# Slab product waits by node chunk, and convolved slabs stay in a buffer on the chip

## The reference

```
xc = attention over channels(x);  xt = attention over time(xc)
s  = softmax(left @ xt^T / sqrt(dk))             # 512 x 512 per sample
h  = einsum('bnm,bmct->bnct', s * A, xt)         # graph product with adjacency A
y  = relu(conv2d(h @ W_gcn, tcn_w) + conv2d(x, res_w))
z  = (y - mean) / sqrt(var + 1e-5) * ln_g + ln_b # over the 16 output channels
```

## Time and profile before

| | |
|---|---|
| median of three runs | 1605.48 us (1602.06, 1605.48, 1621.79) |
| profiled execution, its own time | 1613.76 us |
| its span, first to last instruction | 1612.0 us |
| PE busy | 1377.9 us (85%) |
| PE weight loads busy | 1145.1 us (71%) |
| DVE busy | 955.3 us (59%) |
| ACT busy | 716.2 us (44%) |
| POOL busy | 591.8 us (37%) |
| mean granted PE clock | 0.895 of 2.4 GHz |
| DMA | 174 MB, mean 108 GB/s |

### The profile page before, as it was taken

How to read it: one execution, slowest core, us unless ns; L and a number is a source line. 1 busy time by engine, 2 the same in 40 slices (tenths; PEclk the granted TensorE clock), 3 DMA queues, 4 the chain that set the end, 5 groups by cost and what they waited for, 6 DMA issues and landing times. The chain is left out here.

```text
span 1612.0 us, 25621 instructions
## 1 busy us (share of the span) xinstructions
PE 1377.9 (85%) x8186; PEld 1145.1 (71%) x8202; DVE 955.3 (59%) x2027; ACT 716.2 (44%) x1227; POOL 591.8 (37%) x904
## 2 busy tenths in 40 slices
PE   5788999999398499999999994677899999936997
PEld 5686888878398488888888783666688788833554
DVE  4403788888444764445544433646278888855985
ACT  5432555555154332333333322522255555524996
POOL 1100365665511246655575432100026556560000
PEclk8798999999656699999999995578799999977999
DMA  7461122212276236554574626874112122212321
GB/s 238 123 194 40 40 69 70 77 59 78 75 237 222 88 111 146 105 116 110 124 148 77 123 26 169 294 254 116 40 33 77 59 78 68 61 57 78 102 76 60
DMA packets 105615, 173.99 MB, mean 108 GB/s; under 512 B 14768, under 2 KB 47168, under 8 KB 105540
## 3 DMA queue, kind: packets, MB, share of 16 engines
q1 hardware_dynamic: 83268, 128.95, 25.7%
q0 software_dynamic: 16384, 31.51, 11.3%
q10 hardware_dynamic: 5888, 12.59, 2.2%
HBM read 106.91 MB, written 66.10 MB: 107 GB/s over the span
## 5 line engine op out<-in xcount | busy, mean ns | idle before, releaser
L929 PE MATMUL g_y<-L_z,L_pt 128*128 128x192 f32 x1024 | 198.4, 338 | 1.5 <-ACT L_pt L1144 0.5
L929 PEld LDWEIGHTS g_y<-L_z,L_pt 128*128 128x128 f32 x1024 | 168.0, 194 | 6.8 <-ACT L_pt L1144 6.8
L1089 POOL TENSOR_TENSOR L_xr<-L_xr,L_lnb 128x192 f32<-128x192 f32 x128 | 105.6, 852 | 171.4 <-DMA L_xr<-x 93.4
L1486 POOL DMA_INDIRECT sums<-x_yo,x_places x64 | 102.9, 1609 | 136.0 <-ACT x_yo L1725 125.9
L1136 ACT ACTIVATE L_e<-g_s,L_nm 128x512 f32<-128x512 f32 x128 | 88.0, 687 | 78.2 <-DVE L_nm L977 77.1
L1096 POOL TENSOR_TENSOR L_t<-L_rstd 128x48 f32<-128x48 f32 x96 | 28.9, 301 | 224.9 <-DVE L_rstd L1031 219.9
L897 PE MATMUL g_z<-L_kw,L_xnT 96*128 96x192 f32 x512 | 91.8, 331 | 20.8 <-DVE L_v L1007 20.5
L897 PEld LDWEIGHTS g_z<-L_kw,L_xnT 96*128 96x128 f32 x512 | 82.3, 189 | 30.0 <-DVE L_v L1007 30.0
L1615 DVE TENSOR_TENSOR x_mid<-ex_g,x_sig 128x480 f32<-128x480 f32 (+1 forms) x48 | 31.4, 654 | 120.2 <-ACT x_sig L1716 120.2
L986 DVE SCALAR_TENSOR_TENSOR L_p<-L_e,L_rl,L_adj 128x512 f32<-128x512 f32 x128 | 99.1, 774 | 4.5
L977 DVE TENSOR_REDUCE L_nm<-g_s 128x1 f32<-128x512 f32 x128 | 87.5, 684 | 22.7 <-PE g_s L906 21.9
(11 more groups left out here) (352 smaller groups left out, 3574.4 us busy)
## 6 DMA issues: line engine op xcount, KB each, us to landing
L_xnT<-xn_rows SPq DMA_DIRECT2D x48, 384.0 KB, 3.4
x<-L_y SPq DMA_DIRECT2D x32, 384.0 KB, 2.9
xn_rows<-L_xnT SPq DMA_DIRECT2D x54, 192.0 KB, 4.1
L_xr<-in_x SPq DMA_DIRECT2D x24, 384.0 KB, 3.5
L_xr<-x SPq DMA_DIRECT2D x24, 384.0 KB, 3.8
L_raw<-xn_rows SPq DMA_DIRECT2D x16, 384.0 KB, 4.9
ff_xa<-x SPq DMA_DIRECT2D x12, 512.0 KB, 4.2
out_x<-ff_yo SPq DMA_DIRECT2D x16, 384.0 KB, 2.6
```

Source lines behind the costliest of these rows:

```text
L929: last = nc.tensor.matmul(out, pt[k % 2][:, P * c:P * c + P], z[q][:, c, :], start=False, stop=(c == NK - 1))
L1089: last = nc.gpsimd.tensor_tensor(v_, v_, gain(s.lnb), ALU.add)
L1486: nc.gpsimd.indirect_dma_start(sums, row(places[e % 2][:, 1, t:t + 1]), yo[t % 4][:, :], None, compute_op=ALU.add).then_inc(sent[t % 4], 16)
```

## The change

- **conv_slab** waits for kw_sb ahead of node chunk 0, and for uv_sb ahead of chunk 2 only.
- **graph_conv** has no output in DRAM. residual writes slab b into s.slabs, a view of s.shared, at columns b x 192 of each node chunk; the address comes from the loop register. The stores, the semaphores sent and the waits for them in residual, relu and at the block's end are gone.
- **normalise** with route on reads the slabs from s.slabs, and has no loads and no waits for them.
- **feed_forward** reads its slabs from s.slabs for the transposes and for its residual. The ring xa, the loads and their waits are gone.
- **build**: x1 and x3 are gone. The shared buffer is made per layer, and in layer 1 outside the convolution's buffers, so that it lives through the feed-forward.

```diff
 # normalise
-        xa = [s.xa0, s.xa1, s.xr0, s.xr1]
+        xa = None if route else [s.xa0, s.xa1, s.xr0, s.xr1]
+        def slab(b, k, h):
+            if route:
+                return s.slabs[:, k, CT * b + HALF * h:CT * b + HALF * h + HALF]
+            return xa[b % 4][:, k, HALF * h:HALF * h + HALF]
...
-                    if b + 4 < B:
+                    if not route and b + 4 < B:
                         load(b + 4)
...
                 def turn_slab(b):
-                    pe.wait_ge(xa_in[b % 4], (b // 4 + 1) * 16)
+                    if not route:
+                        pe.wait_ge(xa_in[b % 4], (b // 4 + 1) * 16)
                     since(pe, xn_done, b - D + 1)
...
-                                                       xa[b % 4][:, k, HALF * h:HALF * h + HALF], s.ident[:, :])
+                                                       slab(b, k, h), s.ident[:, :])
 # graph_conv
                 with sp.Fori(0, B // 2 - 2) as i:
                     for q in range(2):
                         load(i * 2 + q + 3, 1 - q)
-                        store(i * 2 + q, q)
                         load_residual(i * 2 + q + 2, q)
...
-                for q in range(2):
-                    sp.wait_ge(sent[q], dma_ready(B // 2 - 1))
...
                 def conv_slab(b, q):
-                    pe.wait_ge(uv_sb, ready(b))
+                    pe.wait_ge(kw_sb, ready(b))
                     for k in range(NK):
+                        if k == 2:
+                            pe.wait_ge(uv_sb, ready(b))
                         for h in range(2):
...
-                def residual(b, q, i):
+                def residual(b, q):
                     dve.wait_ge(gained, ready(b))
                     dve.wait_ge(base_done, ready(b))
-                    dve.wait_ge(sent[q], dma_free(i))
-                    nc.vector.tensor_tensor(y[q][:, :, :], dv[q][:, :, :], xr[q][:, :, :], ALU.add).then_inc(out_done, 1)
+                    nc.vector.tensor_tensor(s.slabs[:, :, bass.ds(b * CT, CT)], dv[q][:, :, :], xr[q][:, :, :],
+                                            ALU.add).then_inc(out_done, 1)
...
                     act.wait_ge(out_done, free(b, 2))
-                    act.wait_ge(sent[q], dma_free(i))
                     nc.scalar.activation(slab(y[q]), psy[:, :, 0:2 * CT], ACT.Relu).then_inc(relu_done, 1)
 # feed_forward
-        xa = [sb(f"xa{z}", [P, NK, W]) for z in range(RING)]
...
                 def turn_slab(b):
-                    pe.wait_ge(slab_in[b % RING], (b // RING + 1) * 16)
                     since(pe, tn_done, b)
...
-                                                       xa[b % RING][:, k, P * h:P * h + P], s.ident[:, :])
+                                                       s.slabs[:, k, W * b + P * h:W * b + P * h + P], s.ident[:, :])
...
-                            in_time(xa[b % RING][:, :, P * h + at:P * h + at + C * count]), ALU.add)
+                            in_time(s.slabs[:, :, P * n + at:P * n + at + C * count]), ALU.add)
 # build
+    def shared_buffer(ctx, L):
+        s.shared = sb(ctx, f"shared{L}", [P, B * NK * CT])
+        s.slabs = s.shared[:, :].rearrange("p (k x) -> p k x", k=NK)
...
-            graph_conv(nc, s, "g0", rows(xn_rows), by_partition(d["x"]), by_partition(x1))
-            normalise(nc, s, "n1", by_partition(x1), 1e-5, rows(xn_rows), keep=rows(raw_rows))
+            graph_conv(nc, s, "g0", rows(xn_rows), by_partition(d["x"]))
+            normalise(nc, s, "n1", None, 1e-5, rows(xn_rows), keep=rows(raw_rows))
```

More of the change, by code:

```diff
@@ L379, in load @@
                 def load(b):
-                    since(sp, logits_done if route else slab_turned, b - 3)
+                    since(sp, slab_turned, b - 3)
                     sp.dma_start(xa[b % 4][:, :, :], src[b]).then_inc(xa_in[b % 4], 16)
@@ L384, in _ @@
                     consts.first(sp)
-                load(0)
-                load(1)
+                if not route:
+                    load(0)
+                    load(1)
                 if consts:
                     consts.rest(sp)
-                load(2)
-                load(3)
+                if not route:
+                    load(2)
+                    load(3)
                 for b in range(B):
@@ L423, in logits @@
                         for k in range(NK):
-                            last = nc.tensor.matmul(psl[0:HALF, at:at + E], xa[b % 4][:, k, HALF * h:HALF * h + HALF],
+                            last = nc.tensor.matmul(psl[0:HALF, at:at + E], slab(b, k, h),
                                                     s.wr[:, k, :], start=(k == 0), stop=(k == NK - 1))
@@ L781, with graph_conv @@
 CENTRE_STEPS, NORM_STEPS = 3, 6
-def graph_conv(nc, s, tag, xn_rows, x_in, x_out, prefetch=None):
+def graph_conv(nc, s, tag, xn_rows, x_in, prefetch=None):
     with ExitStack() as ctx:
-        (xn_in, xr_in, sent, kron_done, kw_done, kw_sb, uv_done, uv_high, uv_sb, z_done, z_sb,
+        (xn_in, xr_in, kron_done, kw_done, kw_sb, uv_done, uv_high, uv_sb, z_done, z_sb,
          score_done, nmax_done, expd, probs, probs_turned, probs_turned_sb, y_done, relu_done, stats_done,
@@ L795, in graph_conv @@
             tag,
-            "xn_in*2 xr_in*2 sent*2 kron_done kw_done kw_sb uv_done uv_high uv_sb z_done z_sb "
+            "xn_in*2 xr_in*2 kron_done kw_done kw_sb uv_done uv_high uv_sb z_done z_sb "
             "score_done nmax_done expd probs probs_turned probs_turned_sb y_done relu_done stats_done "
@@ L841, in _ @@
                         load(i * 2 + q + 3, 1 - q)
-                        store(i * 2 + q, q)
                         load_residual(i * 2 + q + 2, q)
                 load(B - 1, 1)
[L845 to L848, removed]
-                for q in range(2):
-                    sp.wait_ge(sent[q], dma_ready(B // 2 - 1))
+                for b in range(B - 2, B):
+                    load_residual(b, b % 2)
             def item_turns(eng, turn):
@@ L1059, in turn @@
                     if total:
-                        residual(b - 2, q, i - q)
+                        residual(b - 2, q)
                     if norm:
@@ L1159, in turn @@
                     if norm:
-                        relu(b - 1, r, i)
+                        relu(b - 1, r)
                     if softmax:
@@ L2042, in _ @@
             def _(sp):
[L2043 to L2047, removed]
+                for b in range(B):
                     sp.wait_ge(out_done, last_tile(b) + 1)
                     sp.dma_start(x_out[b], yo[b % SLABS][:, :, :]).then_inc(sent[b % SLABS], 16)
[L2051 to L2054, removed]
-                    while done < B and last_tile(done) <= 2 * c + 1:
-                        store(done)
-                        done += 1
-                    if c + RING < STEPS:
-                        load(c + RING)
                 for z in range(SLABS):
@@ L2469, in build @@
     raw_rows = sums[0:TOKENS, :]
-    x1, x2 = (dram(n, [B, P, NK * CT]) for n in ("x1", "x2"))
-    x3 = dram("x3", [P, NK * TOKENS])
+    x2 = dram("x2", [B, P, NK * CT])
     gate_rows = dram("gate_rows", [3 * TOKENS, 1])
@@ L2532, in build @@
                 small_attention(nc, s, "t1", False)
-                graph_conv(nc, s, "g1", rows(xn_rows), by_partition(x2), x3.rearrange("p (k b x) -> b p k x", k=NK, b=B))
-            feed_forward(nc, s, x3.rearrange("p (k j x) -> j p k x", k=NK, x=2 * P), node_major(out))
+                graph_conv(nc, s, "g1", rows(xn_rows), by_partition(x2))
+            feed_forward(nc, s, node_major(out))
         s.sems.ctx.close()
```

17 lines of the change are left out of this document (7 added, 10 removed).

## The result

The changed kernel took 1554.89 us (median of 4 runs, 1552.27 to 1557.21), the kernel before 1603.77 us beside it (4 runs, 1599.72 to 1621.79): a ratio of 0.967 with a 95% interval of 0.960 to 0.975. The forecast was 1563, the range 1548 to 1586. The profiled execution took 1557.21 us (span 1555.4), 56.6 less than that of before.

| stretch | before, us | after, us | saved | the prediction's term |
|---|---|---|---|---|
| begin of g0 to its last residual | 305.2 | 296.5 | 8.8 | 6.3 |
| last residual of g0 to the begin of n1 | 2.8 | 0.3 | 2.5 | 2.5 |
| n1 to the next block's first issue | 79.7 | 50.9 | 28.7 | 26 |
| n1 to the begin of g1 (unchanged) | 623.2 | 621.4 | 1.8 | 0 |
| begin of g1 to its last residual | 305.0 | 297.0 | 8.0 | 6.3 |

What follows compares the result with a forecast made beforehand. PE was taken as tightest in the turns, and in n1 PE-bound at 1.2 GHz; 12.5 + 2.5 + 26 + 6.9 = 47.9 us off 1613.8 gave 1565.9, less a third of 8.3, 1563 us; range 1548 to 1586.

Steps and rivals of the forecast that it cites:

- The turns: Graph convolution turns, both layers: splitting conv_slab's wait fills PE's gap before the product; 12.5 us saved.
- 12 x 0.42: Steady turns 2 to 13 of a layer: each gains 0.42 us, limited by ACT's copy of probability tile 3.
- Turns 0 and 1: First two turns of each layer's convolution: without residual, each gains the whole 0.61 us.
- the store of 2.5 us: End of layer 0's convolution: without the store's landing the next block begins 0.3 us after the last residual; 2.5 us saved.
- n1, 26 predicted: Row norm without its 16 loads: PE stays at 2.4 GHz, 2.75 us a slab; 26 us saved.
- The granted clock came back some 40 us later: Row norm before the change: after a 3.10 us wait for a load, PE's full clock returned some 40 us later.
- while PE worked through at full pace it kept the clock: Row norm: reason given for PE staying at 2.4 GHz once the waits for loads go.
- cold n1: Rival, row norm: PE stays at 1.2 GHz, 5.2 us a slab, a loss of 5 us; 1594 us, chance 0.06.
- The feed-forward: Its begin: no store to land (3.1 us) and no load before the first transposes (3.8 us); 6.9 us saved.
- The third that I took off: Forecast total: a third of the profiled run's 8.3 us above the median, taking 1565.9 to 1563 us.
- came back at other waits: Rival, turns: PE's 0.68 us return in full at spread(b,3) or projections, the 12.5 us go; 1575 us, chance 0.14.
- Residual by a register's address: Rival, DVE: residual's write in four runs is slow and delays 28 turns; 1619 us at 2.0 more, chance 0.03.

Runs made afterwards that it cites:

- buffer alone: Changed kernel with conv_slab's wait for uv_sb back at its start, so that slabs kept on chip are all that is new: 1570.1 us, ratio 0.978.
- Experiment 1: Kernel before with only conv_slab's wait split: 1587.0 us; changed kernel with the old wait back at conv_slab's start: 1570.1 us.
- experiment 2: Changed kernel with 16 slab loads in n1 that nothing reads: 1565.5 us with PE not waiting, 1584.9 us with PE waiting for each.
- experiment 3: Changed kernel with PE stopped in n1 until an unread 49 KB load lands: once 1568.9 us, three times 1576.8 us.
- experiment 4: Changed kernel without the two products per slab that n1 makes only to keep PE busy: 1571.1 us, ratio 0.977.
- wait alone: Kernel before with one edit, conv_slab waiting for kw_sb at its start and uv_sb ahead of chunk 2: 1587.0 us, ratio 0.987.
- experiment 5: Changed kernel with residual later on DVE 1551.3 us, half of conv_slab earlier on PE 1557.6 us, both 1552.2 us; changed kernel beside the last 1561.0 us.
- bytes alone: Changed kernel with 16 slab loads in n1 that nothing reads and PE does not wait for: 1565.5 us, ratio 0.972.
- one gap: Changed kernel with PE stopped once in n1, behind the logits of slab 4, until an unread 49 KB load lands: 1568.9 us, ratio 0.976.
- loads awaited: Changed kernel with 16 unread slab loads in n1, PE waiting for each before that slab's transposes: 1584.9 us, ratio 0.987.

## Why the prediction was right

**The turns, 12.5 predicted, 16.8 measured: mechanism right, size off in the first turns.** From first to last residual, which the steady turns set, 5.3 and 5.7 us were saved, and the working gives 12 x 0.42 = 5.0 for them. The step that was mis-sized is "Turns 0 and 1 have no residual, so there I take the whole 0.61". In g1, from the product of turn 0 on, two products lay 16.86 us apart before and 15.99 after (1170.00 to 1186.86; 1128.18 to 1144.17): 0.87. PE's idle time of 0.61 leaves out that a product behind a pause takes 2.87 in place of 2.77 us, and that, with no pause, it starts 0.16 us before the modelled end of its predecessor. Turns 0 and 1 so gave 1.8 us a layer and not 1.2. The last 2.3 of the 16.8 us lie ahead of turn 0's split of u, and the change does not explain them: from the begin of the convolution to that split the buffer alone, with the old wait, took 25.1 and 27.9 us in its two layers, the kernel before 27.8 and 27.6, and the changed kernel 26.2 and 27.0. Experiment 1 shows that the wait, and not the store, made the turns' gain. A mean turn of 16.49 us stands against 16.45 predicted. That fit hides a miss: the limit has two parts, spread(b,3), as argued, and row_probs(b,2) behind centre on DVE, which the prediction did not have.

**Residual at 0.95 us, the store of 2.5 us: right** (0.95 and 2.5).

**n1, 26 predicted, 28.7 measured: right, with a slab of 2.70 in place of 2.75 us.** The block took 50.9 us where about 53 was predicted. That the load's wait and not only its bytes made it slow is shown by experiment 2, and that a pause alone ends the 2.4 GHz by experiment 3. Two sentences of the working did not hold. "The granted clock came back some 40 us later" was one execution: other runs had 7 to 44 us. And "while PE worked through at full pace it kept the clock" is true only of the work as it stood. In experiment 4 it fell, without a pause, once transposes and narrow logits were all that PE did, and the whole n1 took 15.9 us more. So the two idle products per slab, which the change left alone, carry about half of what was saved from the last residual of g0 to the end of n1 (15.9 of 31.2 us), and the prediction priced a cold n1 without naming them. The Trainium skill ("TensorE: Matmul & The Clock Gate", "Part 4: PE-mode transpose") says that the full clock does not come on for transposes. Against that page, the clock rose behind the first 24 transposes in the changed kernel and in experiment 4, as in the earlier trace rows; for it speaks the fall in experiment 4, so it bears on this case more than I allowed.

**The feed-forward, 6.9 predicted, 8.1 measured.** The transposes follow the last residual after 0.70 us, where 7.54 passed: 6.8, as worked out. The other 1.3 us lie in the stage itself (158.6 to 157.3 us from the first transposes on) and are no gain of the change: the wait alone, with the old feed-forward, took 157.2 us there.

**The sum.** 1613.8 - 47.9 - 2.8 = 1563; with the terms as measured, 4.3 + 2.7 + 1.2 us less, it is 1554.9, the median. To the tenth that is luck, since the stretches that the change leaves alone moved by 1.3 and 1.8 us. The third that I took off for the profiled execution's excess over the median fits what experiment 1 showed, an n1 that in one execution took 10 us less than in another; that this is the whole of the excess is not shown.

**The rivals.** Of the 0.87 us that a pause cost, only 0.4 came back at other waits in a steady turn. The cold n1 did not come, but experiment 4 shows that it was two products per slab away (67.2 us in place of 51.3). Residual by a register's address cost nothing.

## What to carry to other kernels

A wait that holds a whole group of products back for an operand of half of them can be split, here at no cost that a run shows, but look at what the next engine allows: here a steady turn kept 0.47 of the 0.87 us, and two moves together (experiment 5) freed only 0.2 more. A transfer that PE waits for can cost far more than its length, since the pause can take the clock with it; count the work at 1.2 GHz behind it, from several executions. And before idle products on PE are cut, take the clock's rows with and without them.

## What was unexpected of the hardware

- Counted from the end of a pause of PE, the granted clock stayed at 0.50 under work without a pause for very different times: some 7 us (473 to 480 in the bytes alone), 13 (wait alone), 13 (one gap), 39 (before) and 44 (loads awaited).
- The length of the pause alone did not decide. Around 1.84 us (one gap) and 0.96 us (bytes alone, 473.11) the clock fell; behind 1.37 us (wait alone, 466.29) it stayed at 1.00. Behind 1.43 us it fell 1.5 us later in the kernel before and stayed at 1.00 for 5 us in the loads awaited:

```profile
497.65 1.08 PE L427 MATMUL n_psx<-s_ident,s_shared 128*96 128x128 f32 x8 [1.43 <-DMA L_xr<-in_x]
```

- With transposes and logits of 8 columns as PE's only work, it fell with no pause (experiment 4).
- The queues moved 332 GB/s over 32 us with loads and stores together (experiment 2), against 295 to 300 with stores alone in the changed kernel, where their share was 0.92 to 0.93 and not 1.00.
